# Last cross attention of an eight-stage kernel: random features in four 32-row array tiles

## The reference

```
q, k, v = heads(x Wq^T + bq), heads(ctx Wk^T + bk), heads(ctx Wv^T + bv)
q' = relu(q Wqf^T)            # [b, head, token, 64]
k' = relu(k Wkf^T) * mask
kv = k'^T v                   # [b, head, 64, 16], and the sum of k' over the tokens
out = (q' kv) / (q' ksum + 1e-8), then Wo, bo
```

## Time and profile before

| | us |
|---|---|
| median of 3 runs (lowest, highest) | 952.36 (947.3, 953.65) |
| the profiled execution's own time | 950.55 |
| its span | 948.7 |
| TensorE busy in the span | 843.7 (89%) |
| VectorE, ScalarE, GpSimd busy | 591.0, 414.1, 368.3 |

### The profile page before, as it was taken

One profiled execution on the slowest core, in us unless ns is written; L12 is line 12 of the kernel. 1 busy time (PEld: TensorE's weight loads), 2 busy tenths in 40 slices (PEclk: granted clock), 3 DMA queues, 4 the chain that ended last, 5 costly groups with the idle time before them and its releaser, 6 DMA issues.

```text
span 948.7 us, 15615 instructions
## 1 busy us (share of the span) xinstructions
PE 843.7 (89%) x5608; PEld 516.9 (54%) x5608; DVE 591.0 (62%) x1146; ACT 414.1 (44%) x699; POOL 368.3 (39%) x388
## 2 busy tenths in 40 slices
PE   7889898999999868888999689799898999999784
PEld 4466666544276654444454454455557966568431
DVE  4976676245157999888999588795541116113945
ACT  3342332311002778777888536356212343463221
POOL 4333113001013547776777452301150046474335
PEclk9996788799999975555555599889798999997898
DMA  9300001200000009999999900350763142250012
GB/s 310 37 1 0 1 1 38 69 0 1 0 1 1 1 1 178 185 178 172 180 191 191 181 0 1 104 133 2 172 143 122 46 145 84 88 146 28 29 12 34
DMA packets 191901, 76.05 MB, mean 80 GB/s; under 512 B 154161, under 2 KB 189644, under 8 KB 191836
## 3 DMA queue, kind: packets, MB, share of 16 engines
q1 hardware_dynamic: 188892, 69.94, 34.6%
q0 software_dynamic: 2944, 5.25, 2.3%
HBM read 33.21 MB, written 8.40 MB: 44 GB/s over the span
## 4 chain that ended last, share of the span: by engine, by line
PE 56%; DVE 17%; DMA 11%; POOL 5%; issue 4%; ACT 4%; SPq 0%; POOLq 0%; ACTq 0%; DVEq 0%
DMA hT<-hT 11%; PE psum L446 7%; POOL hT L1048 4%; PE psum L483 4%; PE psum L1543 3%; PE psum L596 3%; PE psum L612 3%; PE psum L450 2%; PE psum L1232 2%; PE psum L2040 2%; PE psum L604 2%; PE psum L1826 2%; PE psum L337 2%; PE psum L2022 2%; PE psum L426 2%
## 5 line engine op out<-in xcount | busy, mean ns | idle before, releaser
L1112 DVE TENSOR_REDUCE am<-psum 128x1024 f32 (+1 forms) x128 | 154.9, 1221 | 20.6 <-PE psum L958 17.3
L1048 POOL TENSOR_SCALAR hT<-arena 128x1024 f16<-128x1024 f32 x128 | 134.3, 1049 | 62.0 <-DMA hT<-hT 32.2
L1021 ACT ACTIVATE arena<-psum,am 128x1024 f32<-128x1024 f32 x128 | 142.6, 1114 | 33.7 <-POOL hT L1048 23.9
L958 PE MATMUL psum<-arena 96*128 96x512 bf16 x256 | 130.0, 612 | 16.5 <-ACT arena L1021 12.2
L320 POOL TENSOR_TENSOR rstd<-ve,neg_half 128x1 f32<-128x1 f32 x64 | 39.4, 619 | 215.2 <-DVE ve L310 215.0
L969 PEld LDWEIGHTS psum<-arena,hT 128*128 128x128 f16 x512 | 51.6, 114 | 51.0 <-DMA hT<-hT 24.5
L969 PE MATMUL psum<-arena,hT 128*128 128x16 f16 x512 | 58.5, 185 | 9.9 <-DMA hT<-hT 9.9
L970 PEld LDWEIGHTS psum<-arena,m 128*128 128x128 f16 x512 | 49.4, 115 | 30.1 <-issue 29.9
L663 POOL TENSOR_TENSOR arena<-arena,mask 128x1024 f32<-128x1024 f32 x16 | 30.1, 1904 | 68.5 <-PE psum L596 68.5
L970 PE MATMUL psum<-arena,m 128*128 128x16 f16 x512 | 53.1, 174 | 0.0
L971 PE MATMUL psum<-arena,hT 128*128 128x16 f16 x512 | 53.0, 174 | 0.0
(11 more groups left out here) (388 smaller groups left out, 1849.4 us busy)
## 6 DMA issues: line engine op xcount, KB each, us to landing
hT<-in_L_ffn_expert_masks SPq DMA_DIRECT2D x32, 256.0 KB, 2.9
arena<-in_L_ffn_w_gate SPq DMA_DIRECT2D x2, 1408.0 KB
arena<-in_L_ffn_w_up SPq DMA_DIRECT2D x2, 1408.0 KB
arena<-in_L_ffn_w_down SPq DMA_DIRECT2D x2, 1408.0 KB
moe_in<-xT SPq DMA_DIRECT2D x2, 1024.0 KB, 6.9
hT<-hT SPq DMA_TRANSPOSE x128, 3.3
hT<-moe_in SPq DMA_DIRECT2D x4, 512.0 KB, 5.4
moe_out<-arena SPq DMA_DIRECT2D x16, 128.0 KB, 1.7
```

Of the source, the lines that this page charges most:

```text
L958: mm = pe.matmul(psum[:, score_banks(c), :][:, g, :], QT[0:SPLIT, c % H, bass.ds(row_tile(j, c) * P, P)], KT[0:SPLIT, c % H, g * HALF:(g + ...
L1021: act.activation(PE1[:, c % 2, :], psum[:, score_banks(c), :].rearrange("p a b -> p (a b)"), ACT.Exp, bias=am[:, bass.ds(n, 1)], accum_out ...
L1048: pool.tensor_scalar(Y1[:, n % Y_SLOTS, :], PE1[:, n % 2, :], 255.0, 1024.0, ALU.mult, ALU.add)\
L1112: dve.tensor_reduce(am[:, bass.ds(n, 1)], psum[:, score_banks(c), :], AX.XY, ALU.max, negate=True)\
```

## The change

- Key features (`keys`) take a pair of batches at once. Each product contracts over 32 rows, which hold one pair of heads, stationary 32 x 128 tokens of `kT3`, moving 32 x 128 of `kBD`; the four row groups write four banks of `ring_a`. All four banks are claimed before the first product. ScalarE's relu writes with a stride, `kp` holds two batches per buffer, and its second buffer lies in `cx`.
- Key-value products of two batches follow each pair.
- Query features use 32-row stationaries and 32-row moving operands. Row groups 0 and 1 write banks of `ring_a` (ScalarE's relu), 2 and 3 banks of `ring_v` (VectorE's relu). The order becomes: four features, two mask turns, four times over; then outputs 0 to 3, then outputs 4 to 7 with a turn each.
- The zeroing of `acc3` (which is `cx`) moves on GpSimd from early in the third feed-forward to behind the last key-value product and the masks; `claim` gets an argument for a bank further ahead.

```diff
-    def claim(self, pe):
+    def claim(self, pe, ahead=0):
...
+        n = self.filled + ahead
+        if n >= len(self.banks):
+            pe.wait_ge(self.evacuated, n - len(self.banks) + 1)
+        return self.banks[n % len(self.banks)]
...
-        kp = [a.tile([T]), sg.rearrange("p a b -> p (a b)")]
+        kp = [a.tile([2, T]), cx.rearrange("p (b k) n -> p b (k n)", b=2)]
...
-            def keys(b):
-
-                for c in range(DC):
-                    bank = ring_a.claim(pe)
-                    mm = pe.matmul(bank, kT3[:, c, b * S:(b + 1) * S], kBD.rearrange("p h f -> p (h f)"), start=True, stop=True)
-                    ids["kp", b] = ring_a.fill(mm)
+            def keys(p):
+
+
+                banks = [ring_a.claim(pe, r) for r in range(4)]
+                mms = {}
+                for k in range(2):
+                    for c in range(DC):
+                        for r in range(4):
+                            rows, b = slice(32 * r, 32 * r + 32), 2 * p + k
+                            mms[r] = pe.matmul(banks[r][:, (k * DC + c) * P:(k * DC + c + 1) * P], kT3[rows, c, b * S:(b + 1) * S],
+                                               kBD[rows, 2 * r:2 * r + 2, :].rearrange("p h f -> p (h f)"), start=True, stop=True)
+                for r in range(4):
+                    ids["kp", p] = ring_a.fill(mms[r])
...
-            for b in range(NB + 1):
-                if b < NB:
-                    keys(b)
-                if b >= 1:
-                    keys_values(b - 1)
+            for p in range(NB // 2 + 1):
+                if p < NB // 2:
+                    keys(p)
+                if p >= 1:
+                    keys_values(2 * p - 2)
+                    keys_values(2 * p - 1)
...
-                bank = ring_a.claim(pe)
                 r = pr % 4
-                mm = pe.matmul(bank, qBD[:, 2 * r:2 * r + 2, :].rearrange("p h f -> p (h f)"), qT3[:, pr // 4, g * HALF:(g + 1) * HALF],
-                               start=True, stop=True)
-                ids["qp", g] = ring_a.fill(mm)
+                ring = (ring_a, ring_v)[r // 2]
+                bank, rows = ring.claim(pe), slice(32 * r, 32 * r + 32)
+                mm = pe.matmul(bank, qBD[rows, 2 * r:2 * r + 2, :].rearrange("p h f -> p (h f)"),
+                               qT3[rows, pr // 4, g * HALF:(g + 1) * HALF], start=True, stop=True)
+                ids["qp", g, r // 2] = ring.fill(mm)
...
+            for i in range(2):
+                for pr in range(4 * i, 4 * i + 4):
+                    features(0, pr)
+                turn_at(turn_masks_pe, pe, "features", 2 * i)
+                turn_at(turn_masks_pe, pe, "features", 2 * i + 1)
+            for i in range(2):
+                for pr in range(4 * i, 4 * i + 4):
+                    features(1, pr)
+                for k in (2 * i, 2 * i + 1):
+                    turn_at(turn_masks_pe, pe, "both", k)
             for i in range(4):
-                features(0, 2 * i)
-                features(0, 2 * i + 1)
-                turn_at(turn_masks_pe, pe, "features", i)
-            for i in range(4):
-                features(1, 2 * i)
-                features(1, 2 * i + 1)
                 outputs(i)
-                turn_at(turn_masks_pe, pe, "both", i)
...
+            act.wait_ge(sig("km_ready"), NB)
+            for p in range(NB // 2):
+                if p >= 2:
+                    act.wait_ge(ring_v.full, ids["kv", 2 * p - 3])
+                for r in range(4):
                     bank = ring_a.take(act)
-                    ring_a.release(act.activation(kp[b % 2][:, c * 512:(c + 1) * 512], bank, ACT.Relu))
+                    part = kp[p % 2].rearrange("p b (c r n) -> p (b c) r n", c=DC, r=4)[:, :, r, :]
+                    ring_a.release(act.activation(part, bank.rearrange("p (k n) -> p k n", n=P), ACT.Relu))
...
         def xa3_dve(dve, step):
+            for g in range(2):
+                for i in range(2):
+                    for pr in (4 * i + 2, 4 * i + 3):
+                        bank = ring_v.take(dve)
+                        ring_v.release(dve.tensor_scalar(qpT[:, pr, g * HALF:(g + 1) * HALF], bank, 0.0, None, ALU.max))
...
         def consts3_pool(pool):
             done = sig("consts3")
-            pool.wait_ge(sig("km_ready"), NB)
-            pool.memset(acc3, 0.0).then_inc(sig("acc3_zeroed"), 1)
...
             pool.wait_ge(ring_v.full, ids["kv", NB - 1])
+            pool.memset(acc3, 0.0).then_inc(sig("acc3_zeroed"), 1)
```

More of the change, by code:

```diff
@@ L64, in __init__ @@
         self.filled = self.taken = 0
-    def claim(self, pe):
-        if self.filled >= len(self.banks):
-            pe.wait_ge(self.evacuated, self.filled - len(self.banks) + 1)
-        return self.banks[self.filled % len(self.banks)]
+    def claim(self, pe, ahead=0):
[3 more added lines that the diff above has]
+        return self.banks[n % len(self.banks)]
     def fill(self, last_matmul):
@@ L1781, in xa3_pe @@
             pe.wait_ge(sig("wf_ready"), 2)
-            def keys(b):
-                for c in range(DC):
-                    bank = ring_a.claim(pe)
-                    mm = pe.matmul(bank, kT3[:, c, b * S:(b + 1) * S], kBD.rearrange("p h f -> p (h f)"), start=True, stop=True)
-                    ids["kp", b] = ring_a.fill(mm)
+            def keys(p):
[9 more added lines that the diff above has]
+                    ids["kp", p] = ring_a.fill(mms[r])
             def keys_values(b):
-                pe.wait_ge(ring_a.evacuated, ids["kp", b])
+                pe.wait_ge(ring_a.evacuated, ids["kp", b // 2])
                 pe.wait_ge(sig("mask_ready"), 1)
@@ L1794, in keys_values @@
                 for pr in range(8):
-                    mm = pe.matmul(bank[:, pr * 2 * HA:(pr + 1) * 2 * HA], kp[b % 2][:, pr * P:(pr + 1) * P],
+                    mm = pe.matmul(bank[:, pr * 2 * HA:(pr + 1) * 2 * HA], kp[b // 2 % 2][:, b % 2, pr * P:(pr + 1) * P],
                                    vaug[:, b, 2 * pr:2 * pr + 2, :].rearrange("p h d -> p (h d)"), start=True, stop=True)
                 ids["kv", b] = ring_v.fill(mm)
-            for b in range(NB + 1):
-                if b < NB:
-                    keys(b)
-                if b >= 1:
-                    keys_values(b - 1)
+            for p in range(NB // 2 + 1):
[4 more added lines that the diff above has]
+                    keys_values(2 * p - 1)
             for i in range(2):
@@ L1812, in features @@
             def features(g, pr):
-                bank = ring_a.claim(pe)
                 r = pr % 4
-                mm = pe.matmul(bank, qBD[:, 2 * r:2 * r + 2, :].rearrange("p h f -> p (h f)"), qT3[:, pr // 4, g * HALF:(g + 1) * HALF],
-                               start=True, stop=True)
-                ids["qp", g] = ring_a.fill(mm)
+                ring = (ring_a, ring_v)[r // 2]
[3 more added lines that the diff above has]
+                ids["qp", g, r // 2] = ring.fill(mm)
             def outputs(t):
-                pe.wait_ge(ring_a.evacuated, ids["qp", t // 4])
-                if t == 0:
-                    pe.wait_ge(ring_v.evacuated, ids["kv", NB - 1])
+                pe.wait_ge(ring_a.evacuated, ids["qp", t // 4, 0])
+                pe.wait_ge(ring_v.evacuated, ids["qp", t // 4, 1])
                 bank = ring_v.claim(pe)
@@ L1880, in xa3_act @@
             for g in range(2):
[L1881 to L1887, removed]
+                for i in range(2):
+                    for pr in (4 * i, 4 * i + 1):
+                        bank = ring_a.take(act)
+                        ring_a.release(act.activation(qpT[:, pr, g * HALF:(g + 1) * HALF], bank, ACT.Relu))
+                    for k in (2 * i, 2 * i + 1):
+                        turn_at(turn_masks_act, act, "both" if g else "features", k)
             for i in range(4):
@@ L2015, in ff3_pe @@
                 for i, x in enumerate(xnat):
[L2016 to L2019, removed]
+                    banks = [ring_a.claim(pe, c) for c in range(DC)]
                     for t in range(NB):
```

## The result

The changed kernel takes **963.15 us** (median of 4 runs, 959.27 to 965.37) against 951.81 us (4 runs, 947.30 to 953.65) for the kernel before: ratio **1.0183**, 95% interval [1.0133, 1.0232], slower. Its profiled execution took 964.91 us, span 963.2, against 950.55 and 948.7. (Every ratio here leaves out disturbed executions of both sides, among them one of 1170.56 us and seven of b3's twelve, its profiled one included, while every median counts all, so a ratio is not always the quotient of the medians.)

What follows compares the result with a forecast made beforehand. It took TensorE's own time to bound the kernel. Key stage +6.0, behind it +1.0, query features 0 and outputs +8.5 made +15.5 on the profiled 950.55 us: 966 us, range 946 to 971 (own case 962 to 970.5).

Steps and rivals of the forecast that it cites:

- Key stage: Key features in four row tiles with key-value products: clock falls to half after the first gap; +6.0 us taken.
- the early fall: Key features and key-value products: clock falls at the end of the second set, 36.2 us in all, +8.0.
- The gain of 7.1 us: Key features and key-value products if TensorE keeps the full clock throughout: -7.1 us.
- Behind it: Two mask turns and sixteen transposes after the key-value products may still run at half clock: 0 to +2.5, +1.0 taken.
- Query features at nothing: Query features with eight mask turns: TensorE's 9.8 us saved all goes into waiting for GpSimd, 17.5 us to last turn; 0.
- The warning that the copies out of PSUM may become the bound: Query features: by the skill, splitting the copies over ScalarE and VectorE would pay, -4.4 us; the prediction took 0 instead.
- Outputs: Eight output batches with no streams between them run at half clock: +8.5 us taken.
- full-half case: Output batches at half clock throughout: +6.6 for the first four, +2.8 for those with turns, +9.4 us.
- keys fall, outputs as today: Rival: key features and key-value products at half clock, output batches unchanged; about +7, 957.5 us; chance 0.05.
- serialized tiles: Rival: row tiles do not run concurrently, sets of 3.5 us, keys +2.3, query features +2.4, 955 us; chance 0.05.
- the clock holds: Rival: no fall before the output batches, 943.5 us, or 937 if they too stay at 2.4 GHz; chance 0.16.
- key stage keeps 2.4 GHz: Rival: key features and key-value products at full clock, -7.1, output batches at half, +8.5; 952 us; chance 0.16.

Runs made afterwards that it cites:

- b3: Changed kernel with edited ScalarE waits, idle wide products, and query features, mask turns and outputs mixed one by one; 947.99 us, ratio 0.9941 to the kernel before.
- e1: Changed kernel with its query part as before, so only the key stage is new, and ScalarE's last limits read by eight loads; 958.35 us, ratio 1.0024.
- e4: c2 with GpSimd multiplying only 2 x 32 of 2 x 256 mask columns from the fifth expert on; 963.01 us, ratio 1.0123 to the kernel before.
- e2: Kernel before with only the query part changed, and ScalarE's last limits read by eight loads; 967.07 us, ratio 1.0167.
- c0: Control: kernel before with only ScalarE's eight last waits taking their count from a second register; 951.97 us, ratio 1.0008.
- c2: Control: changed kernel with ScalarE's eight last waits taking their count from a second register; 972.39 us, ratio 1.0219 to the kernel before.

## Why the prediction was right

**Key stage: right in this trace, by the early fall.** The gap behind the first set was 2.26 us, with ScalarE the releaser (2.7 predicted); a set took 1.17 us (1.08); the clock fell at the end of the second set, so four pairs at half made 35.9 us, where the prediction's early case had 36.2. I had taken +6.0 between the cases; it was +7.6. All six traces with this stage bare ran it at half, e1 with nothing else changed, but in five of them the clock was down before the stage began. So the gap as what brings the fall rests on one trace, and b3 fell at the same place with the gap filled. And in time the key part alone is worth 1.5 us with some 6 of uncertainty: +6.0 is borne out by the traces, not yet by the executions. (The 1.08 us a set is 1.06 by its own sum, and the 0.0285 in its bracket comes from no row; neither matters beside the 1.17.) The gain of 7.1 us that the full clock would give was not seen in any trace: the stage never got under 27.1 us, and there with idle products added.

**Behind it: right.** +0.7 for +1.0: the transposes began at half, and the clock was back at their end (823.7).

**Query features at nothing: right.** The last of the eight turns ended 17.57 us after the start of the first set, 17.5 predicted, and GpSimd was the cause. TensorE was busy 11.01 us of it, not about 8, partly because the clock was at half from 840.8 to 844.2, but that lay under the waits. GpSimd's waits and products in the changed kernel, 834 to 852 us, with what VectorE waited, say it from both sides:

```profile
DVE arena L1944 <- PE psum L1826: 23.2, 4, 14.8
PEld psum L1746 <- POOL hT L1911: 10.2, 6, 2.0
PE psum L1746 <- POOL hT L1911: 6.6, 5, 1.8
POOL hT L1911 <- PE psum L1746: 3.2, 1, 3.2
```

TensorE waits for GpSimd at five turns; VectorE's new relus (687 ns each) have 23.2 us of room. The warning that the copies out of PSUM may become the bound after such a gain (the Trainium skill, TensorEngine Tiling (Array Packing), Performance Considerations) did not describe this kernel; it comes near the truth only in e4, where ScalarE is busy 8.91 of 10.13 us once GpSimd's share is gone.

**Outputs: right in kind, 1 us short.** They ran at half from first to last. Features and outputs together took 17.57 + 30.53 us against 38.45, +9.65, where the prediction's full-half case said +9.4 and I took +8.5. e2 shows that the query part alone brings this, in its trace and in time (1.0167).

**What the sum hid.** The stages of the prediction came to +17.95 us, where it had +15.5; that the profiled execution was only 14.4 us slower than the one before (964.91 against 950.55), and the median, 963.15, under the 966 forecast, is luck in part. Two things are off by more than the total shows. The work ahead of the key stage, the same in both kernels, came out 3.1 us shorter in the changed kernel's trace; starts in the table run from 784.0 to 793.6, so a sum over one execution cannot be better than some microseconds. And the +9.65 was taken against a trace in which the old outputs had themselves fallen to half. Against c0, where they had not, the query part costs 46.6 - 33.2 = 13.4 us in the trace of c2. The rival "keys fall, outputs as today" is refuted by e2, "serialized tiles" by the 1.17 us set, and "the clock holds", as "key stage keeps 2.4 GHz", by the granted clock of 0.50 in the key stage of each trace of the change.

**The cause of the fall is only in part shown.** What is shown: it comes with the new stages, at half they do not get the clock back as the old key stage did, the outputs' fall is not GpSimd's pace alone (e4), and it outlasts the waits. The falls within the 7 us pauses fit the rule that idle gaps between bursts bring the half clock (the Trainium skill, TensorE: Matmul & The Clock Gate, HAM oscillation). The gap of 2.26 us before the key stage's fall in the changed kernel is shorter than the gaps of which that section speaks. And b3 fell in 30.46 us that were busy to the last 0.01, right behind 8.40 busy us, while c0 held 1.00 through outputs of the same narrow kind. Neither idle time nor narrow products alone tell when it falls.

## What to carry to other kernels

When a change makes TensorE's wide products short, price what is left at both clock levels, for more than the saved time may come back through the narrow products that remain: here 14 us of products less in each of two stages came out, in the profiled executions, as 8 us more in the keys and 10 more in query features and outputs. Look for the engine that paces the stretch before moving work off TensorE (here GpSimd's 1.27 us products): b3's order spreads them beside the outputs instead of ahead of them, and its stretch was the shortest of all. And take the clock from several executions of the unchanged kernel before calling one of its falls a property of the code.

## What the runs showed beyond that

- Four concurrent 32-row fp32 tiles of 128 columns: 32 instructions in 1.17 us at the full clock, 2.02 at half; the 512-column form, eight instructions in 1.07 to 1.14 us, broken up by other products 1.13 for four.
- ScalarE can stand still for 2.5 to 5.9 us between two evictions whose data lies ready, at the same place of its program, in eleven of fourteen traces; the cause stays open.
- The kernel before, unchanged, spread from 937.75 to 965.61 us in the runs beside the experiments, apart from one.
